# Three narrow late steps: moving five heads of a layer's score maxima in a two-layer cross-attention kernel

## The reference, cut to what matters

```
layer 0:  q, text k, v (77 rows), image k, v (298 rows)
          out = softmax(q k_text) v_text + softmax(q k_image) v_image;  x = out Wo + bo + x
layer 1:  q from layer 0's x; text k, v (371 rows), image k, v (4 rows)
          p = softmax(q k_text);  text_out = p v_text
          sem = cosine(p context, image context);  fused = q k_image + 0.5 sem
          ip_out = softmax(fused) * mask * v_image;  x = (text_out + ip_out) W + b + x
```

## Time and profile before

| what | value |
|---|---|
| median of 3 runs | 2549.21 us (2546.79 to 2550.13) |
| the profiled execution, its own time | 2540.84 us |
| its span in the trace | 2539.1 us |
| granted TensorE clock, mean | 0.995 of full speed |
| busy: PE, PEld, DVE, ACT, POOL | 97%, 84%, 64%, 48%, 30% |
| chain that ended last | PE 77%, DVE 13%, POOL 4% |

### The profile page before, as it was taken

The page is one execution under the profiler, slowest core; times in us unless marked ns, Lnnn a source line. Parts: engine busy times, 40 slices in busy tenths (PEclk is TensorE's granted clock), DMA queues, the critical chain, the costliest instruction groups (busy, mean ns, idle before and its releaser), DMA issues.

```text
span 2539.1 us, 64279 instructions
## 1 busy us (share of the span) xinstructions
PE 2462.1 (97%) x26500; PEld 2130.7 (84%) x26500; DVE 1633.7 (64%) x3217; ACT 1226.5 (48%) x2251; POOL 768.8 (30%) x998
## 2 busy tenths in 40 slices
PE   8899999999999999999999999999999999999998
PEld 7788888888888888888888888888888888888877
DVE  4465667766667655667656677656677556676665
ACT  3355445455444454444554444554454554444543
POOL 3133223233233233233332333332332332332322
PEclk9999999999999999999999999999999999999999
DMA  9765446674546754556655466655566644556621
GB/s 213 140 107 86 89 87 97 103 120 73 87 88 97 116 90 84 89 90 111 103 88 89 86 105 98 107 79 87 97 95 105 96 81 89 89 98 102 95 27 20
DMA packets 373418, 241.47 MB, mean 95 GB/s; under 512 B 133675, under 2 KB 366971, under 8 KB 373116
## 3 DMA queue, kind: packets, MB, share of 16 engines
q1 hardware_dynamic: 373126, 237.36, 57.1%
HBM read 171.35 MB, written 64.59 MB: 93 GB/s over the span
## 4 chain that ended last, share of the span: by engine, by line
PE 77%; DVE 13%; POOL 4%; SPq 2%; DMA 2%; issue 2%; ACT 1%; DVEq 0%; POOLq 0%; ACTq 0%
PE ST L820 7%; PE R L886 5%; PE R L762 5%; PE PN L859 5%; PE R L775 4%; PE R L776 4%; PE R L707 4%; DVE m L1068 4%; PE R L708 4%; POOL w L1444 4%; PE R L944 3%; PE R L778 3%; PE PN L904 3%; PE R L710 3%; PE R L891 3%; PE R L889 3%
## 5 line engine op out<-in xcount | busy, mean ns | idle before, releaser
L1444 POOL TENSOR_TENSOR w<-w 128x448 f32<-128x448 f32 (+1 forms) x256 | 331.1, 1293 | 378.8 <-DVE w L977 360.6
L980 DVE SCALAR_TENSOR_TENSOR w<-p,pr 128x1344 f32<-128x1344 f32 x160 | 296.3, 1852 | 163.8 <-ACT pr L1330 151.0
L1302 ACT ACTIVATE p<-ST 128x1344 f32<-128x1344 f32 x260 | 335.5, 1290 | 103.9 <-PE ST L823 99.5
L977 DVE TENSOR_TENSOR rem<-R,kst 128x298 f32<-128x298 f32 (+2 forms) x180 | 89.4, 497 | 431.1 <-ACT kst L1185 431.1
L886 PE MATMUL R<-pr,Gh 128*128 128x448 f32 (+1 forms) x960 | 366.2, 381 | 0.0
L977 DVE TENSOR_TENSOR w<-R,w 128x448 f32<-128x448 f32 (+1 forms) x480 | 281.4, 619 | 68.6 <-PE R L891 58.0
L1378 POOL TENSOR_TENSOR kst<-rem,kst 128x298 bf16<-128x298 f32 (+2 forms) x180 | 148.0, 822 | 535.6 <-ACT kst L1185 296.4
L775 PE MATMUL R<-wvh,ch 128*128 128x320 f32 (+3 forms) x896 | 302.9, 338 | 1.9 <-DVE rem L977 1.9
L776 PE MATMUL R<-wvh,cl 128*128 128x320 f32 (+3 forms) x896 | 277.4, 310 | 0.0
L820 PE MATMUL ST<-Qs,Ks 100*128 100x112 bf16 (+1 forms) x3520 | 229.3, 214 | 12.0 <-DMA Qs<-ms 4.9
L820 PEld LDWEIGHTS ST<-Qs,Ks 100*128 100x128 bf16 (+1 forms) x3520 | 188.0, 98 | 50.5 <-issue 14.1
(11 more groups left out here) (221 smaller groups left out, 5930.3 us busy)
## 6 DMA issues: line engine op xcount, KB each, us to landing
Ks<-k_split SPq DMA_DIRECT2D x384, 140.6 KB, 5.7
Ks<-k_split SPq DMA_DIRECT2D x384, 93.8 KB, 8.1
w<-in_ctxT SPq DMA_DIRECT2D x31, 750.0 KB, 9.9
k_split<-kst SPq DMA_DIRECT2D x64, 281.2 KB
k_split<-kst SPq DMA_DIRECT2D x64, 223.5 KB, 2.9
Qs<-q_split SPq DMA_DIRECT2D x64, 210.0 KB, 8.7
q_split<-qst SPq DMA_DIRECT2D x128, 84.0 KB, 2.4
Qs<-q_split SPq DMA_DIRECT2D x64, 140.0 KB, 8.7
```

The lines of the kernel that those rows point to most:

```text
L977: return e.tensor_tensor(to, x, y, op)
L980: return e.scalar_tensor_tensor(out=to, in0=x, scalar=s, in1=y, op0=op0, op1=op1)
L1302: e.activation(to.rearrange("p (u q) -> p u q", u=3), st, ACT.Exp).then_inc(p_whole, 1)
L1444: e.tensor_tensor(first, first, w2[n % 2][0:ROWS[j], QW * j:QW * j + QW], ALU.add).then_inc(ns_added, 1)
```

## The change

Layer 1's maxima of heads 15 to 19 leave the stretch. They become three narrow steps (heads 15 and 16; 17 and 18; 19 alone), which stand among the first two groups of the next pass's layer 0 scores. `m_T` of layer 1 goes from behind the scores' group 0 to behind group 2, `m_split` from behind group 1 to behind group 3. In the stretch, layer 0's `m_T` and `m_split` both come right after the first step of layer 1, and the pieces are placed at other counts. All of it holds for passes 1 to 30 (stretch) and 2 to 31 (late steps), 30 each; the other passes keep their order.

```
+ALL_STEPS = [(h + d, n, d == 0) for h in range(0, H, 5) for d, n in ((0, 3), (3, 2))]
+NOW_STEPS = ALL_STEPS[0:6]
+LATE_STEPS = [(15, 2, False), (17, 2, False), (19, 1, False)]
...
+    def max_step(b, l, h0, n, wide):
+        key = (b, l, h0, n, wide)
+        o.add("s_max", *key)
+        o.max_steps[b, l] = o.many["s_max"]
+        for part in ("ST",) if wide else ("PV", "NS"):
+            o.share(part, 1, ("s_max", b, l, h0), "s_max_read", o.at("s_max", *key))
...
+    def defers(b):
+        return SETS_FROM <= b + 1 < B
...
+        late = iter(LATE_STEPS if b and b < B and defers(b - 1) else ())
+        def late_step():
+            for step in islice(late, 1):
+                max_step(b - 1, 1, *step)
...
         def among0(g):
-            take(rows1, 1)
+            if b < B and defers(b - 1):
+                late_step()
+                take(rows1, 1 if g > 1 else 0)
+            else:
+                take(rows1, 1)
...
             take(pieces, 1 if b + 1 < B and (b or g < 4) else 0)
+            late_step()
...
         def between():
             count[0] += 1
-            if count[0] > 9:
+            if defers(b):
+                take(rows0, 2 if count[0] == 9 else 0)
+            elif count[0] > 9:
                 take(rows0, 1)
             if count[0] in (1, 2, 3, 5, 7, 9, 10):
                 take(last, 1)
-            if count[0] in (2, 4, 6, 8, 11, 12, 14, 16):
+            if count[0] in ((1, 3, 5, 6, 8, 9, 11, 13) if defers(b) else (2, 4, 6, 8, 11, 12, 14, 16)):
                 take(pieces, 1)
...
-            rows1 = maxima(b, 1, between)
+            rows1 = maxima(b, 1, NOW_STEPS if defers(b) else ALL_STEPS, between)
...
-                    w.wait_ge(s_max_read, 8 * at("m_T", b, l))
+                    w.wait_ge(s_max_read, o.max_steps[b, l])
```

More of the change, by code:

```diff
@@ L1 @@
 from contextlib import ExitStack
+from itertools import islice
 import concourse.bass as bass
@@ L37, in __init__ @@
         self.ring, self.slot, self.freed = {}, {}, {}
+        self.max_steps = {}
     def add(self, kind, *key):
@@ L148, in ahead, with maxima @@
         yield from tail
[L150 to L159, removed]
+    def max_step(b, l, h0, n, wide):
[4 more added lines that the diff above has]
+            o.share(part, 1, ("s_max", b, l, h0), "s_max_read", o.at("s_max", *key))
+    def maxima(b, l, steps, between):
+        for step in steps:
+            max_step(b, l, *step)
+            between()
         return m_rows(b, l)
@@ L334, in among @@
             warm("R", n)
-    rows0 = maxima(0, 0, among)
+    rows0 = maxima(0, 0, ALL_STEPS, among)
     flush()
@@ L424, in stage_order @@
         if b + 1 < B:
-            rows0 = maxima(b + 1, 0, between)
+            rows0 = maxima(b + 1, 0, ALL_STEPS, between)
             take(rows0, 1)
@@ L791, in tensor @@
                 elif kind == "s_max":
-                    b, l, h0, wide = key
-                    n, to = (3, ST) if wide else (2, PN)
+                    b, l, h0, n, wide = key
+                    to = ST if wide else PN
                     w.wait_ge(d_kr[l][0 if h0 + n <= HALVES[0][1] else 1], 96 * (b + 1))
```

## The result

The changed kernel took 2583.42 us in the median of four runs (2576.75 to 2587.03), beside 2548.0 us before. The ratio is 1.0141, with a 95% interval from 1.0128 to 1.0155: 35 us slower. The forecast was 2597, 48 slower.

A forecast was written before the change was run, and what follows sets the result against it. PE was taken as the bound, busy 74.02 of 76.13 us a pass; 0.55 + 1.34 - 0.30 = 1.59 us a pass, times 30, 48 us, added to 2549.21 gave 2597 us, range 2560 to 2622.

The forecast's parts named there:

- Work: Whole pass: same 40 maxima matmuls on PE, one more layer 1 step for DVE, taken as 0.
- N15's wait: First late step, behind scores 0: PE waits for PN until DVE has read N13, 0.55 us a pass.
- N19's wait: Third late step, behind scores 1: N17's read follows DVE's key tile share; PE waits 1.16 or 1.51 us, mean 1.34.
- The stretch: Stretch of maxima: PE's waits fall from 1.92 to 1.60 us, a gain of 0.3 us a pass.
- only waits change: Stretch of maxima: same work less five heads (0.8 us, made again at the late steps), so only waits differ.
- The sum: Whole pass: the two late waits less the stretch's gain, 1.59 us a pass slower, 48 us over 30 passes.
- Faster, since DVE's full stretch is relieved: Rival, stretch: with DVE's reads taken away its waits go, at best 58 us less, 2491 us; chance 0.08.
- Late DMAs: Rival, layer 0 scores: six small DMAs land after scores are due, 1 us more a pass, 2627 us; chance 0.07.
- The clock: Rival: PE's waits of up to 1.5 us cost 2 us of full clock a pass, 2627 us; chance 0.03.

The follow-up runs named there:

- Experiment 5: Kernel before's stretch order with the last value product behind N13, the five heads at the late steps, N19 behind the queries; 2538.88 us, ratio 0.9975.
- Experiments 2 to 5 and 9: Changed kernel with last value product behind N13, 2587.8 us; that plus N19 behind the queries, 2548.11 us; and Experiment 4, Experiment 5, experiment 9.
- Experiment 1: Changed kernel with N19 moved behind the queries and layer 1's m_T behind the second key tile; 2546.51 us, ratio 0.9995.
- Experiment 4: Changed kernel's late steps, but the kernel before's stretch order with the last value product behind N13; 2576.46 us, ratio 1.0123.
- Experiment 6: Experiment 1 with the stretch's first value product behind N3 again, as in the kernel before; 2534.47 us, ratio 0.9956.
- experiment 9: experiment 7 with the last two value products each one step later, behind the narrow steps; 2493.22 us, ratio 0.9784.
- experiment 8: experiment 7 with the third g moved behind N13, the last thing before the scores; 2684.26 us, ratio 1.0546.
- experiment 7: Experiment 6 with ip_T behind the value product that followed it and layer 0's m_T behind o_T; 2508.57 us, ratio 0.9854.

## Why the prediction was right, step by step

**Work: right.** The forecast took nothing for the extra step. Experiment 5 has it, and no late wait, and is no slower than before.

**N15's wait: right.** 0.55 was forecast. In the shown pass PE is done with the scores at about 988.82 (start 988.23 and some 0.59 for its twelve matmuls) and starts N15 at 989.39, 0.57. Experiments 2 to 5 and 9 took it away, by more work between the two narrow steps.

**N19's wait: right, and in both sizes.** The trace has 29 such waits in its table, in two sizes, 15 of 1.01 and 14 of 1.36 us idle. With the 0.17 by which a matmul's modelled end lies behind PE's last issue they are 1.18 and 1.53, where 1.16 without and 1.51 with DVE's rounding of the key tile were forecast. Experiment 1 shows that this wait is worth 37 us. How much of it is DVE's order was read from the rows, not tried by itself; but the two sizes, 0.35 apart, are the rounding: the 15 shorter ones stand in passes in which ACT does it.

**The stretch: near in the number, wrong in where it comes from.** 0.3 a pass was forecast, 0.45 measured as the mean and 0.35 in most passes (24.31 before, 23.16 after, with the 0.80 taken out). The mean is larger for passes in which the kernel before had a longer stretch, one of them 26.43. The ledger held for DVE: N3's read starts 2.91 into the stretch (2.92 forecast) and W5's ends at 6.63 (6.51). But the waits of PE that it led to were put too small. By starts, in the shown pass, W10 waits 1.20 (1.0), `ip_T` 0.30 (0.30), `m_T` 0.37 (0.25) and the scores 0.10 (0.05); N13 and `o_mm` don't wait. That is 1.97, or 1.9 with W10's mean over the run, where 1.60 was forecast and 1.92 stood before. The waits gave back nothing; they only changed places. The prediction said that "only waits change", and that step failed: what the stretch gained is small gaps that its ledger didn't list. In the kernel before, a narrow step that has waited spends 0.21 between its two matmuls and not 0.16, three times in the stretch:

```profile
950.57 0.32 PE L804 MATMUL PN<-Ks,Qs 96*112 96x375 bf16 x1
```

N18 of layer 1 waited 0.06 for N13's read, `o_T` and `m_T` took 0.06 more together, and the products of `o_mm` 1.68 up to the next step where they now take 1.61. Together these are about 0.34 a pass. That the number came near is therefore luck. Experiment 4 agrees: with the old order of the stretch nothing is gained but the moved heads. Experiment 6 shows that N3's new place makes part of W10's wait.

**The sum: right in sign, some 12 us too large.** 1.59 a pass was forecast and 1.21 is the mean of the trace (-0.45 and +1.66); times 30 that is 36, and the medians differ by 35. Of the 0.38 a pass that are missing, 0.15 are the stretch. The late waits are 1.93, where 1.89 was forecast, but the rest of the pass has lengthened by 1.66 only: 0.27 were gained there, a term that the prediction had at nothing. One part of it stands in the traces. In 15 of the 30 passes, those in which ACT rounds the rest of the key tile, the kernel before makes scores 2 wait 0.16 longer for `ST` (5.21 behind scores 0 and not 5.05), since the exponentials stand behind that rounding. One such pass:

```profile
744.66 0.46 ACT L1185 ACTIVATE kst<-rem 128x298 bf16<-128x298 f32 x1 [0.53 <-DVE rem L977]
745.02 1.27 ACT L1302 ACTIVATE p<-ST 128x1344 f32<-128x1344 f32 x1
746.34 0.71 PE L820 MATMUL ST<-Qs,Ks 102*128 102x112 bf16 x11
```

In the changed kernel these passes differ from the others by N19's shorter wait alone (7.49 and 7.84 behind scores 0): PE comes later than ACT. That is 0.08 a pass. What gives the rest of the 0.27, I have not found; some of it is in passes longer than the usual one.

**The rivals.** "Faster, since DVE's full stretch is relieved" fails on what it took for granted: DVE's busy time in the stretch fell by 2.7 us and PE's waits there not at all (1.92 and 1.97 by starts in the shown passes). They hang on when one read ends, not on how busy DVE is. Late DMAs: the table of waits of the changed kernel has none for them between 160 and 2400 us; experiment 9, with its shorter stretch, comes near it. The clock: 0.995 as before, with waits of up to 1.5 us.

## What to carry to other kernels

With one buffer between two engines that work in order, what counts is the distance from one use to the next, here 1.58 us, and what stands ahead of the read in the reader's own queue. A busy share of 91% said nothing of it, and an idle spell of the reader is of no use where the instruction next in its list waits for a third engine. Put work between two uses of the buffer on the writer's side, none between write and read on the reader's, and when an edit mends one pair, check the pairs that it brings together.

## What the runs showed of the hardware

Waits of 0.4 to 1.5 us by starts, four a pass at the steps and `m_T`, left the granted clock at 1.00 in the windows of the changed kernel. In experiment 8, PE stood for 3.49 us and then ran at a granted 0.50 of full speed, 1.2 GHz: its key matmuls start every 0.25 us instead of every 0.14. That lasted about 3 us, and the clock was 1.00 again by 1030. Twelve such matmuls cost 1.3 us more. From the first scores on, the usual pass got 5.6 us longer than in experiment 7 (6.95 and 1.36 over before): 3.65 of waiting, 1.3 of slow clock and 0.85 of a wait for ACT further on, less N15's 0.57, make 5.2 of it. The Trainium skill (TensorE: Matmul & The Clock Gate, Part 1) says that the clock falls when PE has been idle and returns after it has been busy for a while; this trace agrees, and the changed kernel's shows that its short waits, however regular, were not enough.
